# A Mamba–attention–feed-forward block on one core: units of one sequence, resident weights, dense products in three float32r parts

## The reference

```python
x = x + layernorm(attn_block(layernorm(x)))
x = x + layernorm(ffn_block(layernorm(x)))

def attn_block(x):                       # x0 = x
    xm = (m[0] + m[1]) * x;  n = rms_norm(xm)
    value, gate = split(n @ in_proj_w)   # 2 x 256 channels
    value = silu(causal_conv4(value))
    Bm, Cm = xm @ B_proj_w, xm @ C_proj_w            # 16 heads x 64 states
    y = selective_scan(value, A, Bm, Cm, dt, 64) + D * value
    xm = xm + mamba_scale * (y * silu(gate)) @ out_proj_w
    xm = xm + m_mlp_scale * relu(rms_norm(xm) @ fc)**2 @ proj      # hidden 512
    xa = a[0] * xm + a[1] * x0;  n = rms_norm(xa)
    q, k = rope(rms_norm(n @ q_w)) * q_gain, rope(rms_norm(n @ k_w))   # 16 and 4 heads of 8
    xa = xa + attn_scale * causal_softmax(q k^T / sqrt(8)) v @ o_w
    return xa + a_mlp_scale * relu(rms_norm(xa) @ fc)**2 @ proj

def ffn_block(x):                        # ternary weights, hidden 512
    h = silu(x @ w1.T * s1) * (x @ w2.T * s2)
    h = gelu(h @ h1.T * s_h1);  h = gelu(h @ h2.T * s_h2)          # 512 x 512 each
    return h @ w3.T * s3
```

## Time and profile before

| | |
|---|---|
| median of 3 runs | 1063.42 us (1061.19 to 1063.5) |
| the profiled execution's own time | 1061.02 us |
| its span, first to last instruction | 1059.3 us, so 1.7 us lie outside |
| instructions | 18517 |
| busy: PE, DVE, ACT, POOL | 949.9, 650.2, 527.2, 251.5 us |
| moved by DMA | 32.51 MB |
| mean granted TensorE clock | 0.965 |

### The profile page before, as it was taken

How to read it: one execution, slowest core, us unless ns; L and a number is a source line. 1 busy time by engine, 2 the same in 40 slices (tenths; PEclk the granted TensorE clock), 3 DMA queues, 4 the chain that set the end, 5 groups by cost and what they waited for, 6 DMA issues and landing times.

```text
span 1059.3 us, 18517 instructions
## 1 busy us (share of the span) xinstructions
PE 949.9 (90%) x7008; PEld 585.2 (55%) x7008; DVE 650.2 (61%) x1715; ACT 527.2 (50%) x1123; POOL 251.5 (24%) x410
## 2 busy tenths in 40 slices
PE   1678688698999999999999999999999999689787
PEld 0455454564565756576666656575656655544433
DVE  4955886596676656776686657766667634831311
ACT  3424437546662566437572667247552662273131
POOL 3001104222330423114310523023300511160200
PEclk9899899899999999999999999999999999689989
DMA  7000000000111011110111001101011011002110
GB/s 223 1 1 1 11 2 1 11 2 11 31 31 51 12 30 31 41 31 11 31 40 41 21 21 31 56 16 31 11 41 32 21 40 50 21 11 63 46 43 27
DMA packets 52311, 32.51 MB, mean 31 GB/s; under 512 B 2688, under 2 KB 49024, under 8 KB 52224
## 3 DMA queue, kind: packets, MB, share of 16 engines
q1 hardware_dynamic: 52224, 31.33, 10.1%
HBM read 29.23 MB, written 2.10 MB: 30 GB/s over the span
## 4 chain that ended last, share of the span: by engine, by line
PE 66%; DVE 8%; ACT 3%; issue 1%; POOL 1%; POOLq 0%; DVEq 0%; ACTq 0%
PE bank L1147 54%; PE CB L1147 7%; DVE cv L900 2%; PE bank L1158 2%; DVE mneg L1053 1%; PE bank L1388 1%; PE bank L1346 1%; DVE cv L896 1%; ACT xpad L641 1%; ACT junk L595 1%; PE bank L1302 1%; ACT bnT L602 0%; ACT val L632 0%; POOL relu L522 0%; DVE bn L849 0%
## 5 line engine op out<-in xcount | busy, mean ns | idle before, releaser
L1053 DVE TENSOR_REDUCE mneg<-bank 128x2 f32<-128x512 f32 (+1 forms) x192 | 119.4, 685 | 43.5 <-PE bank L1147 43.4
L914 DVE TENSOR_TENSOR M<-CB,LM 128x512 f32<-128x512 f32 x128 | 87.8, 686 | 87.8 <-PE CB L1147 87.0
L1147 PE MATMUL bank<-hC,slot 128*128 128x512 f32 x256 | 115.6, 599 | 0.0
L1147 PE MATMUL bank<-hD,slot 128*128 128x512 f32 x256 | 114.2, 592 | 0.0
L602 ACT ACTIVATE relu<-bank 128x512 f32<-128x512 f32 x64 | 38.8, 606 | 84.8 <-PE bank L1147 84.3
L1147 PEld LDWEIGHTS bank<-hC,slot 128*128 128x128 f32 x256 | 46.9, 190 | 51.7 <-issue 50.7
L1147 PEld LDWEIGHTS bank<-hD,slot 128*128 128x128 f32 x256 | 47.5, 190 | 50.2 <-issue 49.3
L497 POOL TENSOR_TENSOR oms<-omv,eps_ln 128x4 f32<-128x4 f32 x8 | 1.6, 199 | 286.0 <-DVE omv L843 286.0
L752 ACT ACTIVATE hD<-bank,cols 128x512 f32<-128x512 f32 x32 | 22.0, 688 | 91.9 <-PE bank L1147 91.9
L1147 PE MATMUL CB<-cv,relu 64*128 64x256 f32 (+1 forms) x512 | 59.1, 349 | 6.9 <-DVE M L915 6.8
L1147 PE MATMUL CB<-ct,relu 64*128 64x256 f32 (+1 forms) x512 | 59.8, 352 | 5.7 <-DVE M L915 5.7
(11 more groups left out here) (224 smaller groups left out, 2016.1 us busy)
## 6 DMA issues: line engine op xcount, KB each, us to landing
slot<-in_w_h SPq DMA_DIRECT2D x64, 256.0 KB, 3.0
slot<-in_w SPq DMA_DIRECT2D x16, 256.0 KB, 2.6
xh<-in_x SPq DMA_DIRECT2D x8, 256.0 KB, 2.9
x_res<-in_x SPq DMA_DIRECT2D x8, 256.0 KB, 2.9
out<-out_sb SPq DMA_DIRECT2D x8, 256.0 KB, 2.3
relu<-in_w_B SPq DMA_DIRECT2D x1, 512.0 KB, 5.1
relu<-in_w_C SPq DMA_DIRECT2D x1, 512.0 KB, 5.7
PX<-in_rows SPq DMA_DIRECT2D x1, 320.0 KB, 6.0
```

The costliest lines, as they stand in the source:

```text
L914: v.tensor_tensor(both(M[:, k % 2, r, :, 0:2 * P]), both(CB[:, :, 0:2 * P]), first, ALU.mult)
L1053: v.reduce_max(neg, of, axis=AX.X, negate=True).then_inc(evac("K", n), 1)
L1147: return p.matmul(o, lhsT, rhs, start=start, stop=True, skip_group_check=True)
```

## The change

A unit is one sequence of 256 tokens, 16 units in place of 8 pairs. `TURNS` and `BANKS` are written anew; the scan becomes a chain of its own (S), and the stream of weights is gone.

- The feed-forward weights are loaded once and kept as high and low float32r parts (2.5 MB read once instead of once for every pair). The parts are made in the prologue, high ones by DVE, low ones of the feed-forward by POOL.
- All dense products that were float32 and 512 wide become `split_product` at 256 columns: three float32r products. The input needs a high and a low part. For the outputs of a transposition ACT writes the high part and DVE subtracts the low part out of PSUM (`hi_part`, `lo_part`; the mixer's x had this before). For the hidden layers ACT copies the high part and POOL subtracts the low part (`hd_part`, `hc_part`).
- `bc` makes B and C of a pair of heads for one unit in one bank, six products of 256 columns.
- The scaling of the four RMS norms goes from DVE to ACT (`rms_norm` as an activation with a scale).
- The head norms: DVE sums the squares (128x40), POOL adds epsilon, raises to -0.5 and multiplies the gain (`rope2` on POOL), DVE scales. The Newton steps are gone.
- More buffers: `xh` 3, `xa` 4, `x1` 2, `xmT_hi` and `xmT_lo` 2 each, `Vr` 2, and separate tiles where one was lent.

```diff
-PAIRS = BATCH // 2
-TOK = 2 * L
+UNITS = BATCH
+TOK = L
...
-        def gate1(i, j):
-            if j == 0:
-                wait_evac(pe, "F", i, N_X2)
-                wait_slot(pe, i, 0)
-            project("F", i, N_W + 2 * j, in_slot(i, 0)[:, j, :], x2T[:])
...
-        def hidden(i, n, j, src, ready):
-            wait_slot(pe, i, 2 + n + j - N_H1)
-            w = in_slot(i, 2 + n + j - N_H1)
-            wait_free(pe, "F", i, n + j)
-            for k in range(NBLK):
-                if j == 0:
-                    wait_evac(pe, "F", i, ready(k))
-                last = mm(psum("F", i, n + j), w[:, k, :], src[:, k, :], start=(k == 0))
+        def gate_(i, j):
+            if j == 0:
+                if i == 0:
+                    pe.wait_ge(ffn_lo, 1)
+                wait_evac(pe, "F", i, F_X2)
+            wait_free(pe, "F", i, F_W + j)
+            J = slice(j * P, (j + 1) * P)
+            o = psum("F", i, F_W + j)
+            split_product(block(o, 0), w_1_hi[:, J], w_1_lo[:, J], x2T_hi[:], x2T_lo[:], True)
+            split_product(block(o, 1), w_2_hi[:, J], w_2_lo[:, J], x2T_hi[:], x2T_lo[:], False).then_inc(full("F"), 1)
+
+        def hidden(i, n, b, w_hi, w_lo, x_hi, x_lo):
+            wait_free(pe, "F", i, n + b)
+            for k in range(2):
+                J = slice((2 * b + k) * P, (2 * b + k + 1) * P)
+                for c in range(NBLK):
+                    last = split_product(block(psum("F", i, n + b), k), w_hi[:, c, J], w_lo[:, c, J], x_hi[:, c, :], x_lo[:, c, :], k + c == 0)
...
+        def hd_part(i, b):
+            two = slice(2 * b, 2 * b + 2)
+            pool.wait_ge(S["hd_hi"], at(i, "hd_hi", b + 1))
+            g.tensor_tensor(hD_lo[:, two, :], h[:, two, :], hD_hi[:, two, :].bitcast(F32), ALU.subtract).then_inc(S["hd_lo"], 1)
...
+        def rope2(i, _):
+            pool.wait_ge(S["q_sum"], i + 1)
+            if i > 0:
+                wait_evac(pool, "H", i - 1, H_QKV)
+            g.tensor_tensor(qs[:, 1, :], qs[:, 0, :], eps_q[:], ALU.add).then_inc(S["q_rs"], 1)
+            pool.wait_ge(S["q_rs"], at(i, "q_rs", 1))
+            g.tensor_tensor(qs[:, 2, :], qs[:, 1, :], half_q[:], ALU.pow).then_inc(S["q_rs"], 1)
+            pool.wait_ge(S["q_rs"], at(i, "q_rs", 2))
+            g.tensor_tensor(qs[:, 3, :], qs[:, 2, :], gain[:], ALU.mult).then_inc(S["q_rs"], 1)
...
+        def rms_norm(src, dst, r):
+
+            for k in range(TILES):
+                last = a.activation(dst[:, k, :], src[:, k, :], ACT.Copy, scale=r[:, k:k + 1])
+            return last
```

More of the change, by code:

```diff
@@ L59 @@
-EVACUATED = dict(
[L60 to L67, removed]
-def _scan():
[L72 to L82, removed]
+    bn_n=1, aggr_n=TILES, rs_n_eps=2, rs_n=2, nrm_n=2, xm=1, ssq_n=TILES,
@@ L104, in _chains @@
[L104 to L111, removed]
@@ new lines, in _opened @@
+        down=["Y", 1] if k == 0 else [], n3_turn=["H", H_N3], qkv=["H", H_QKV], qk_turn=["K", K_Q + k], k_turn=["A", A_K],
+        scores=["K"] + [K_S + HKV * k + j for j in range(HKV)], q2_turn=["A", A_TURN + k], wts=["A"] + [A_EXP + HKV * k + j for j in range(HKV)], pv=["PV", k],
+        y_rows=["A", A_YT + k], y_turn=["T", T_Y], o_proj=["B", 0], n4_turn=["T", T_N4], up_b=["T", T_FC + k],
+        down_b=["B", 1] if k == 0 else [], x2_turn=["F", F_X2], gate=["F", F_W + k],
+        hidden1=["F", F_H1 + k], hidden2=["F", F_H2 + k], ffn_out=["FO", 0] if k == 0 else []).get(name, [])
@@ L185, in _banks @@
 def _banks():
-    chains = {c: iter([(name, i, k) for i in range(PAIRS) for name, k in CHAINS[c] if name in PE_ITEMS]) for c in CHAINS}
+    chains = {c: iter([(name, i, k) for i in range(UNITS) for name, k in CHAINS[c] if name in PE_ITEMS]) for c in CHAINS}
     digits, where, before, holder = iter(BANKS), {}, {}, {}
@@ L427, in pipeline @@
     def pipeline(engine, parts):
-        chains = {c: iter([(name, i, k) for i in range(1 if c == "W" else PAIRS) for name, k in CHAINS[c] if name in parts]) for c in CHAINS}
+        chains = {c: iter([(name, i, k) for i in range(1 if c == "W" else UNITS) for name, k in CHAINS[c] if name in parts]) for c in CHAINS}
         for c in TURNS[engine]:
@@ new lines, in val_turn, with bc @@
+        def val_turn(i, _):
+            if i > 0:
+                act.wait_ge(S["y_mm"], at(i, "y_mm", 0))
+            wait_full(act, "M", i, M_XT)
+            for b in range(2):
+                for k in range(TILES):
+                    m = (b * TILES + k) * P
+                    src = psum("M", i, M_XT)[:, m:m + P].rearrange("p (q a c) -> p a q c", a=2, c=PS)
+                    last = a.activation(diag(xpad, k, b), src, ACT.Copy)
+            last.then_inc(evac("M", M_XT), 1)
+        def bc(i, hp):
+            if SCORES * i + hp >= 4:
+                act.wait_ge(S["cb_full"], at(i, "cb_full", hp - 3))
+            copy("S", i, hp, BC[hp % 4][:].rearrange("p m l -> p (m l)"))
@@ new lines, in hidden, with hidden1 @@
+        def hidden(i, n, b, w_hi, w_lo, x_hi, x_lo):
+            wait_free(pe, "F", i, n + b)
+            for k in range(2):
+                J = slice((2 * b + k) * P, (2 * b + k + 1) * P)
+                for c in range(NBLK):
+                    last = split_product(block(psum("F", i, n + b), k), w_hi[:, c, J], w_lo[:, c, J], x_hi[:, c, :], x_lo[:, c, :], k + c == 0)
+            last.then_inc(full("F"), 1)
+        def hidden1(i, b):
+            if b == 0:
+                pe.wait_ge(S["hd_lo"], at(i, "hd_lo", 2))
+            hidden(i, F_H1, b, w_h1_hi, w_h1_lo, hD_hi, hD_lo)
@@ L1458, in ffn_out, with hidden2 @@
+        def hidden2(i, b):
+            if b == 0:
+                pe.wait_ge(S["hc_lo"], at(i, "hc_lo", 2))
+            hidden(i, F_H2, b, w_h2_hi, w_h2_lo, hD_hi, hD_lo)
+        def ffn_out(i, b):
+            if b == 0:
                 wait_free(pe, "FO", i, 0)
-            wait_evac(pe, "F", i, N_H2 + j)
-            last = to_tokens(psum("FO", i, 0), hD[:, j, :], w_3, j)
-            if j == NBLK - 1:
+            wait_evac(pe, "F", i, F_H2 + b)
+            for j in (2 * b, 2 * b + 1):
+                last = to_tokens(psum("FO", i, 0), h[:, j, :], w_3, j)
+            if b == 1:
```

1033 lines of the change are left out of this document (520 added, 513 removed).

## The result

The changed kernel takes 1080.37 us (median of 4 runs, 1079.87 to 1082.72) against 1062.31 us of the kernel before beside it. The ratio is 1.0168, 95% interval 1.015 to 1.0186: slower by 1.7%. The profiled execution has a span of 1078.5 us. The forecast was 1000 us.

A forecast was written before the change was run, and what follows sets the result against it. PE's own work was taken to bound the middle: 882 us for the rounds, 100 for head and tail and 16 of waits gave 998 us of span, with 1.7 outside it 1000 us; range 945 to 1062.

The forecast's parts named there:

- The products: On PE, float32r products of 256 columns cost 0.118 us each, 408 a pair, 48.1 us.
- rival 5: Head and tail halve and PE's products take 0.107 us: 929 us in all; chance 0.05.
- Rival 1: On PE, float32r at 256 columns does not hide its weight load; each 0.01 us costs 33 us; chance 0.07.
- I take 2 to 4: The head norms' power over 128x40 on POOL takes 2 to 4 us, between ends of 1.0 and 8.3.
- rival 2: POOL's power goes by element, so low parts for `hidden1` come late: 48 us more, 1048 us; chance 0.12.
- The waits: PE misses handovers from other engines now and then, tightest from gate to `hidden1`: 1 us a unit, 16 us.
- Head and tail: Start and end of the run, costing 127 us before, fall to 100, between bounds of 64 and 127.
- The other engines: Per pair, DVE comes to about 80 us, ACT to 84, POOL to at least 52, against a round of 110.
- signs I named: Products 0.115 to 0.123 apart, units near 55 us, PE 96 to 99% busy, first full round before 298 us.

The follow-up runs named there:

- e5_lo_on_dve: The changed kernel with the low parts `hD_lo` of both hidden layers computed by DVE instead of POOL, the power staying on POOL: 1102.4 us.
- e2_newton: The changed kernel with the head norms' roots back on DVE by Newton's steps, as in the kernel before, instead of POOL's power: 1064.0 us.

## Why the prediction was wrong

The forecast was 882 + 16 + 100 = 998 us of span; the profile has 16 x 55.7 = 891 of PE's work, 16 x 3.8 = 61 of waits and 126 of head and tail, 1078. Two terms were wrong enough to turn the result round: the power on POOL and the head and tail.

- **The products** were right. They start 0.118 us apart (0.118 taken). No run shows the 0.107 and 0.123 that stand beside it, and with them 847 to 899 for the rounds and rival 5: in the changed kernel the starts within the rows of three lie 0.11 to 0.13 apart, by 0.118 in the mean. At 0.137 the sum would have reached the time before (62 us over 3264 products, on top of 0.118). Without the power's waits and their clock PE's work is 54.7 us a unit, 109.4 a pair, where I had 110.3. Rival 1 is out.
- **The step that failed first is "I take 2 to 4"** for the power over 128x40. It takes 6.78, near the upper end of 8.3 that stood beside it: 0.70 us over 128x2, 1.008 over 128x4, 3.54 over 128x20 and 6.78 over 128x40 lie on 0.39 us and 0.16 a column. The trace of before has the power at one width only, so the slope could not be read from it; but I took a value in the lower half with nothing that spoke for it, and the chance of 0.12 for rival 2 followed from that. Rival 2 was the right mechanism, POOL late behind a power that goes by element. That its 48 us stand so near to the 45 measured by leaving the power out is in part luck: it was priced for 8.3 us and for the wait for `hD_lo`, and the time went into another wait.
- **The waits**, 1 us a unit, are 1.4 without the power: a small error (6 us). With it they are 3.8, and the lower clock puts 1.0 on PE's work (some 0.2 on the round). I had no term for the clock, though the head and tail of before show it at 0.94 and 0.88 where PE is idle for 74 and 31 us. I also looked at one consumer behind the power, the low parts for `hidden1` "2.5 to 3 us late". The larger wait is for the masks of `P`, which stand directly behind it; the low part is 0.7 us late, in every other unit.
- **Head and tail**, taken at 100 us, are 126, as before (127, or 129 by the mean of four rounds). This is the second step that failed, and it is not the power's doing: without the power the same reckoning gives 136. "A second unit can overlap the first sooner and the last unit's serial chain is shorter" did not show: the seventh unit's `xm` starts at 291.0 us, where the fourth pair's, with the same six sequences ahead of it, started at 281.4; and the last two units take 310 us from their first `xm` to the end, where the last pair took 313. PE's idle time went from 74 to 68 us in the head, and from the last `xm` to the end from 32 to 51, with the clock at 0.93 and 0.91. It stayed so in every run: 62 to 70 us in the head, but for 90 with the power doubled, and 45 to 54 in the tail, but for 69. From the last `xm` to the end a unit takes 252 us, 4.2 rounds; a pair took 313, 2.7 of its rounds. The head is in part work that does not halve: PE's first wait, which ends when DVE is through with the decay constants and the first norm, is 14.1 us (17.5 before), and POOL's splitting of weights costs 5.6 us by one run and 1.1, not clear of noise, by another. Why the tail's idle time grew was not tried in a run; its waits are spread over many tiles, the largest for `hD_lo`, and `e5_lo_on_dve`, which moved that, left the tail at 252 us.
- **The other engines** were sized rightly except POOL. Two units in the middle, in the columns of the stretches above:

```profile
410.00:529.00 119.00, 111.28 (x1134) 93.57 (x1133) 85.42 (x232) 81.58 (x188) 61.26 (x80) 0.99 0.03 8
```

  DVE works 85 us (80 forecast), ACT 82 (84), POOL 61 ("at least 52"). None is the bound. What counts is not POOL's 51% but that its 15 us of unbroken work lie where PE wants three of its results.
- Of the signs I named, the first full round came at 291, earlier than the 298 I had written; but 298 was the edge of my stretch, and the same mark of the kernel before lies at 281.4, so this sign was against me too. The unit's 59.5 us instead of 55, PE's 94% instead of 96 to 99, the waits for `hD_lo` and head and tail at 126 were the ones that said it wrong.

Put together, the sum was too low by 9 us of PE's work (7 too high without the clock's 16), 45 of waits and 26 of head and tail: 998 + 80 = 1078. The two bounds that came true both stood in the prediction, 1048 with rival 2 and 127 for head and tail; together they are 1075, slower than before, and I had given that pair no chance of its own. With the power left out the same kernel takes 1035 us against 1062 before, but then it does not compute the roots, which the kernel before does. With the roots by the same Newton's steps on DVE it takes 1064.0, no gain, and with the rotation first 1050.8, 12 us less than before. Against these the power on POOL costs 16 to 30 us, and against no roots at all 45.

## What to carry to other kernels

A long instruction on an engine that is half idle is not hidden by that idleness: the 6.78 us of the power on POOL, 51% busy in the middle, cost 45 us of the run. Look at what stands behind it in its in-order queue and when each of these is wanted; moving one of them ahead showed only the next here (3.24 us for `BC` instead of 1.96 for `P`). When the price of an operation is known at one width alone, do not take the middle of the bounds: work out the forecast at the upper end, and together with the bad ends of the other terms, not one at a time; if it changes sign, the range must say so. And free a bank with the work that does not need the late value (rotate, then scale): beside Newton's steps it was worth 13 us for no instruction more.

## What the runs showed of the hardware

Beside POOL's wide subtractions some of DVE's instructions took longer. In the changed kernel, beside `hD_lo` on POOL (451.87 to 454.62 us):

```profile
452.12 1.38 DVE L1047 TENSOR_TENSOR Qb<-ro,Qb 128x256 bf16<-128x256 f32 x1
453.42 1.29 DVE L1048 TENSOR_TENSOR Kb<-ro,Kb 128x64 bf16<-128x64 f32 x1
```

and the same two in `e2_newton`, where POOL's subtractions had ended at 449.56:

```profile
453.61 0.43 DVE L1060 TENSOR_TENSOR Qb<-ro,Qb 128x256 bf16<-128x256 f32 x1
453.95 0.22 DVE L1061 TENSOR_TENSOR Kb<-ro,Kb 128x64 bf16<-128x64 f32 x1
```

Newton's steps of 0.90 and 1.20 us above fit the same effect. The power did not show it: this addition, beside it (441.69 to 448.46), takes 0.42 us.

```profile
443.76 0.42 DVE L1007 TENSOR_TENSOR xa<-xm,xh 128x256 f32<-128x256 f32 x1
```

In the run without the power this addition takes 0.51 us.

Side by side, beside a wide subtraction and without one: 1.38 and 0.43 us for `Qb`, 1.29 and 0.22 for `Kb`, 0.90 and 1.20 against 0.20 for two of Newton's steps, 4.58 and 0.40 for the convolution step. Not every instruction got longer: a cast to `Kb` that starts at 451.89, beside `hD_lo`, takes 0.19 us, and so does the one at 451.59 ahead of it. No run shows the cause, nor why it was so beside the subtractions and not beside the power.
